# Attention and a pooled non-local block on two images: from eleven fenced stages to one program per engine

## The reference

```python
# layer 0: 8 heads of 32 channels
q, k, v = split(w_qkv @ X)                       # 256 x 4096 each
attn = softmax(q_h.T @ k_h / sqrt(32))           # 4096 x 4096 per head
X = w_proj @ (attn @ v_h) + X
# layer 1: non-local block with pooled keys (1024 = 4096 / 4) and values
g = maxpool2(g_w @ X + g_b)                      # 256 x 1024
theta = theta_w @ X[:64] + theta_b               # 64 x 4096
phi = maxpool2(phi_w @ X[64:] + phi_b)           # 64 x 1024
y = softmax(theta.T @ phi) @ g.T                 # 4096 x 1024, then 4096 x 256
X = batchnorm(W_w @ y.T + W_b) + X
```

## Time and profile before

| | |
|---|---|
| runs | 2638.99, 2633.73, 2636.41 us; median 2636.41 us |
| profiled execution | 2638.56 us, of which the span from first to last instruction is 2636.8 us |
| PE busy | 2511.5 us (95%) |
| ACT busy | 2285.4 us (87%) |
| DVE busy | 2176.7 us (83%) |
| POOL busy | 403.4 us (15%) |
| mean granted PE clock | 0.983 of 2.4 GHz |
| instructions | 59152 |
| instruction queues q8 and q14 | 202 packets with 3.31 MB and 86 packets with 0.70 MB |

### The profile page before, as it was taken

How to read it: one execution, slowest core, us unless ns; L and a number is a source line. 1 busy time by engine, 2 the same in 40 slices (tenths; PEclk the granted TensorE clock), 3 DMA queues, 4 the chain that set the end, 5 groups by cost and what they waited for, 6 DMA issues and landing times. The chain is left out here.

```text
span 2636.8 us, 59152 instructions
## 1 busy us (share of the span) xinstructions
PE 2511.5 (95%) x25066; PEld 722.6 (27%) x25066; DVE 2176.7 (83%) x1420; ACT 2285.4 (87%) x2575; POOL 403.4 (15%) x588
## 2 busy tenths in 40 slices
PE   6999999989999999898969999999899999998999
PEld 3222222232222222244432222222322222222444
DVE  5899999978899999696558999999689999996954
ACT  6999999979999999467469999999699999994664
POOL 0112211201112211110001221222011221121100
PEclk9999999999999999899989999999999999998999
DMA  2556656615556656201125666666155665662011
GB/s 86 113 129 126 125 120 129 126 37 111 115 129 126 125 120 129 56 1 49 42 73 129 122 126 124 126 125 124 30 113 129 126 125 120 129 126 43 1 56 40
DMA packets 85088, 262.65 MB, mean 100 GB/s; under 512 B 17616, under 2 KB 18704, under 8 KB 84528
## 3 DMA queue, kind: packets, MB, share of 16 engines
q0 software_dynamic: 64512, 234.91, 43.7%
q1 hardware_dynamic: 20288, 23.72, 2.7%
HBM read 14.75 MB, written 8.68 MB: 9 GB/s over the span
## 5 line engine op out<-in xcount | busy, mean ns | idle before, releaser
L542 DVE TENSOR_TENSOR acc<-acc,P 128x2048 f32<-128x2048 f32 x704 | 1613.4, 2292 | 79.9 <-ACT P L500 13.4
L500 ACT ACTIVATE P<-scores 128x1536 f32<-128x1536 f32 x1024 | 1596.1, 1559 | 0.0
L420 PE MATMUL psOL<-P,V 128*32 128x512 f32 (+1 forms) x8960 | 1073.1, 567 | 1.4 <-ACT P L500 1.4
L409 PE MATMUL psOL<-Q,K 32*128 32x512 f16 x3072 | 839.9, 379 | 28.8 <-ACT P L499 16.9
L409 PE MATMUL scores<-Q,K 32*128 32x512 f16 x9216 | 846.4, 379 | 0.0
L499 ACT ACTIVATE P<-psOL 128x512 f32<-128x512 f32 x1024 | 713.0, 696 | 36.6 <-PE scores L409 36.6
L567 POOL DMA_DIRECT2D accD<-P x384 | 335.6, 995 | 1229.3 <-ACT P L500 1046.2
L409 PEld LDWEIGHTS psOL<-Q,K 32*128 32x128 f16 x3072 | 207.0, 93 | 984.6 <-ACT P L499 856.5
L420 PEld LDWEIGHTS psOL<-P,V 128*32 128x32 f32 x8960 | 196.5, 108 | 473.9 <-issue 438.0
L409 PEld LDWEIGHTS scores<-Q,K 32*128 32x128 f16 x9216 | 220.0, 92 | 0.0
L564 POOL DMA_DIRECT2D accD<-P x64 | 35.2, 556 | 654.3 <-ACT P L500 371.9
(11 more groups left out here) (128 smaller groups left out, 1705.4 us busy)
## 6 DMA issues: line engine op xcount, KB each, us to landing
accD<-P POOLq DMA_DIRECT2D x448, 512.0 KB, 5.3
X<-in_x SPq DMA_DIRECT2D x16, 512.0 KB, 7.4
out<-res SPq DMA_DIRECT2D x32, 256.0 KB, 2.0
R<-pool_inv SPq DMA_DIRECT2D x2, 2048.0 KB, 7.0
wq<-in_w_qkv SPq DMA_DIRECT2D x1, 768.0 KB, 4.8
Ls<-L SPq DMA_DIRECT2D x32, 8.0 KB
att_inv<-Ls SPq DMA_DIRECT2D x32, 8.0 KB
ww_sb<-in_W_w SPq DMA_DIRECT2D x2, 256.0 KB, 2.8
```

The source lines that it names most:

```text
L409: last = nc.tensor.matmul(dst[h], K[rows, kp, j * 128:(j + 1) * 128], Q[rows, qp, cs], start=(n == 0), stop=(n == 2))
L420: last = nc.tensor.matmul(both[h * D:(h + 1) * D, lo:hi], V[:, j, h * D:(h + 1) * D], P[:, r + h, lo:hi], start=(j == 0), stop=(j == JT - 1))
L500: nc.scalar.activation(P[:, r + 1:r + G, :], bank[n % 2].rearrange("p (u n) -> p u n", n=CH), ACT.Exp, scale=SCORE).then_inc(s_exp, 1)
L542: nc.vector.tensor_tensor(acc[:], old, P[:, r:r + G, :], ALU.add).then_inc(s_add, 1)
```

## The change

There is one block for the whole of both images. Each stage is now a set of functions per engine (`Part`), and each engine runs through them in straight order, for b = 0 and b = 1 written out. Semaphores belong to the program; those of layer 0 and of layer 1 are cleared once by POOL in the middle of the other layer (`clean_first`, `clean_second`). All buffers that came and went are views of one arena with fixed places. The bounds of all four attentions go to `worst`; the flag is computed once at the end, and the branch to a general path that does both images again stands behind the end. At the borders parts are interleaved:

```diff
+        def sync_setup(sp):
+            sp.dma_start(wq32, wqkv.rearrange("(t p) o -> p t o", p=128)).then_inc(s_wq, 16)
+            for c in range(3):
+                load_x(sp, 0, c)
+            ...                       # the other weights, then X chunks 3 to 7
+        def scalar_setup(act):
+            act.wait_ge(s_wq, 16)
+            nc.scalar.activation(wq[0][:], wq32, ACT.Copy, scale=WS).then_inc(s_wqs, 1)
...
+                for c in range(NC):                    # projection, tensor
+                    unit(c, 0)
+                    if c == 0 and between:
+                        between(pe)                    # sums_of_acc, _tile, _dma of the attention before
...
+                low(0)                                 # projection, vector
+                if between:
+                    between(dve)                       # sums_out of the attention before, or results(NC - 1)
...
+                pe.wait_ge(s_nx, 2 * NC - 1)           # attention, tensor
+                pe.wait_ge(s_ev, 2 * NC - 2)
+                pe.wait_ge(s_ve, NC - 1)
+                scores(0, 0)
...
+            def room(act):                             # before Xh of the next projection is written
+                for m in range(NC * JT - RING, NC * JT - RING + 5):
+                    slot_free(act, m)
...
+                    if c == NC - 1 and following:      # attention, sync
+                        sp.wait_ge(s_ready, NC * JT)
+                        following(sp)                  # inverted sums of chunks 0 to 6 from DRAM
...
+                if between:                            # layer 1, tensor
+                    pe.wait_ge(behind.signals["exp"], 2 * NC * JT)
+                broadcast(0)                           # into two banks of scores6
+                if between:
+                    between(pe)                        # sums_of_acc, _tile, _dma
...
+                    if c == 1:                         # layer 1, vector: moved behind chunk 0
+                        for n in range(NG):
+                            dve.wait_ge(homes[n], 16 * NC if b is not None else 16)
+                        nc.vector.reciprocal(Ls[:, :, NC - 1, :], Ls[:, :, NC - 1, :]).then_inc(s_rec, 1)
...
+                for c in range(NC):                    # layer 1, sync
+                    for t in range(CT):
+                        sp.wait_ge(s_res, c * 2 + t + 1)
+                        sp.dma_start(out_v[dram, :, t, c * CH:(c + 1) * CH], res[:, t, :]).then_inc(s_st, 16)
+                    if following is not None:
+                        load_x(sp, following, c)
...
+            def _(act):
+                scalar_setup(act)
+                for b in range(B):
+                    if b:
+                        act.wait_ge(s_clean, CLEAN * b - 1)
+                        act.sem_inc(s_past, 1)
+                    project[0].scalar(act, 16 * (b + 1), None, (layer1.signals["yf"], CT * NC + 2) if b else None)
+                    if b == 0:
+                        scalar_weights(act)            # cw high, moved out of the setup
+                    attend[0].scalar(act)
+                    project[1].scalar(act, None, attend[0].signals["room"], None)
+                    attend[1].scalar(act)
+                    ...
+                    layer1.scalar(act, b)
...
+        end_phase(once + first_sems + layer1.sems)
+        known_safe = nc.values_load(safe[0:1, 0:1], min_val=0, max_val=1)
+        with nc.If(known_safe < 1):
+            with nc.Fori(0, B) as b:
+                general(b)
```

More of the change, by code:

```diff
@@ L1 @@
+from collections import namedtuple
 from contextlib import ExitStack
@@ new lines, in conv_seq @@
+        s_cw = sem(root, "s_cw")
+        s_sq0 = sem(root, "s_sq0")
+        s_bn = sem(root, "s_bn")
+        s_clean = sem(root, "s_clean")
+        s_past = sem(root, "s_past")
+        s_x = [sem(root, f"s_x{c}") for c in range(NC)]
+        loads = [(wp_sb[:], wproj.rearrange("(t p) o -> p t o", p=128)),
+                 (gw_sb, gw.rearrange("(t p) o -> p t o", p=128)),
+                 (col[:, :, 0:6], vectors.rearrange("(t p) k -> p t k", p=128)),
+                 (tb_sb[:], biases)]
@@ new lines, in gpsimd_setup, with vector_setup @@
+        def gpsimd_setup(pool):
+            nc.gpsimd.memset(ident[:], 0.0).then_inc(s_id, 1)
+            pool.wait_ge(s_id, 1)
+            nc.gpsimd.affine_select(out=ident[:], in_=ident[:], compare_op=ALU.not_equal, fill=1.0,
+                                    base=0, pattern=[[-1, 128]], channel_multiplier=1).then_inc(s_id, 1)
+        def vector_setup(dve):
+            nc.vector.memset(cw32[:, :, 0:CM], 0.0).then_inc(s_zero, 1)
+            nc.vector.memset(pw_sb[:, 0, :], 0.0).then_inc(s_zero, 1)
+            nc.vector.memset(ones[:], 1.0).then_inc(s_sp, 1)
+            nc.vector.memset(spread[:], 0.0).then_inc(s_sp, 1)
+            nc.vector.memset(heads[:], 0.0).then_inc(s_hd, 1)
+            dve.wait_ge(s_hd, 1)
+            for h in range(G):
+                last = nc.vector.memset(heads[h * D:(h + 1) * D, h * D:(h + 1) * D], 1.0)
+            last.then_inc(s_hd, 1)
+            dve.wait_ge(s_wqs, 1)
+            nc.vector.scalar_tensor_tensor(out=wq[1][:], in0=wq32, scalar=WS, in1=wq[0][:],
+                                           op0=ALU.mult, op1=ALU.subtract).then_inc(s_wqs, 1)
@@ new lines, in conv_seq, with clean_first, clean_second @@
+        project = [projection(g) for g in range(NG)]
+        attend = []
+        for g in range(NG):
+            attend.append(attention(g, project[g], attend[-1] if attend else None))
+        layer1 = second_layer(attend[-1], [a.signals["out"] for a in attend])
+        first_sems = [s for p in project + attend for s in p.sems]
+        def clean_first(pool):
+            for s in first_sems:
+                pool.sem_clear(s)
+            pool.sem_inc(s_clean, 1)
+        def clean_second(pool):
+            for s in layer1.sems:
+                pool.sem_clear(s)
+            pool.sem_inc(s_clean, 1)
@@ L1237, in layer1 @@
[L1237 to L1243 removed]
+                        layer1.signals["rows"](sp, b)
+                        for n in range(NG):
+                            sp.dma_start(Ls[:, n, NC - 1, :], L[0:128:D, :]).then_inc(attend[n].signals["out"], 16)
```

1865 lines of the change are left out of this document (971 added, 894 removed).

## The result

| | kernel before | changed kernel |
|---|---|---|
| median of the runs | 2636.25 us (2633.73 to 2638.99, 4 runs) | 2572.63 us (2569.51 to 2573.57, 4 runs) |
| profiled execution | 2638.56 us | 2573.04 us |
| its span | 2636.8 us | 2571.3 us |
| PE busy | 2511.5 us, 95% | 2501.2 us, 97% |

Ratio of after to before: 0.9756, 95% interval 0.9744 to 0.9767. The gain is 63.6 us by the medians and 65.5 by the two profiled executions; 74.9 were forecast. 2572.6 lies inside the range, 11.6 us above the predicted 2561 and just outside the likeliest case's own range (2552 to 2571).

The account below looks back on a forecast made before the run. Stages are bound by busy PE and ACT, so only PE's rests at borders can shrink: 11.0 + 6.9 + 18.9 + 25.4 + 18.1 = 80.3, less 5.4 gives 74.9 us, from median 2636.4 to 2561; range 2551 to 2580.

Parts of the forecast that it names:

- likeliest case: Whole kernel: the border gains come as reckoned, giving 2561 us, own range 2552 to 2571; chance 0.78.
- Start: Kernel's beginning, once: weights waited for singly and X loaded early, so PE starts at 9.0 instead of 19.97; gain 11.0 us.
- projection to attention: Four borders: scores wait only for an earlier reduction instead of a meeting, so exponentials start sooner; gain 6.9 us in all.
- image border: Image 0 to image 1, once: PE goes straight on at full clock with X already split; gain 18.1 us.
- Attention 0 to projection 1: Two borders: 17.5 us from last values to regular pace becomes 8.1, with flag and branch moved to the end; gain 18.9.
- Attention 1 to layer 1: Two borders: from last values to third residual 13.1 us instead of 26.4 and 25.2; gain 25.4 together.
- sums (3.1) to +4.4: Attention 1 to layer 1: after broadcast 0, the sums take 3.1 us and end 4.4 us behind the last values.
- End: After the last store: more clears 1.1 us, flag's load 0.5, jump over the general path 3.8; cost 5.4 us.
- the code, not the jump: Rival at stage borders: ACT's 3.8 us pause is fetching new code, which the straight program keeps; 2584 us, chance 0.06.
- loads before stores: Rival in image 0: queued X loads delay stores and so DVE and PE, 3 us per chunk; 2585 us, chance 0.04.
- partly: Rival: a wait at two of nine borders lasts as long as the meeting did, 10 to 14 us less; 2573, chance 0.08.
- the clock: Rival in the four attentions: unbroken PE work drops the clock to 1.2 GHz; 2677 us at 6%, chance 0.02.

Follow-up runs that it names:

- e7: Changed kernel with image 1's inputs loaded only after image 0's last store landed, and the last results ahead of the projection's first low part on VectorE; 2580.35 us.
- e4: Kernel before without its general path and the branch to it, stages and meetings as they were; 2620.21 us against 2638.11.
- e5: Changed kernel with the attention's sums put back ahead of the projection's first unit at the border from attention 0 to projection 1; 2568.92 us.
- e1: Changed kernel with the attention weights' rows of chunk 0 read back while attention 1's last chunk still runs; 2571.26 us.
- e10: e1 with rows of chunks 0 to 2 read at the start of attention 1's last chunk, 3 to 6 only behind the sums' copy; 2562.33 us.
- e3: Changed kernel without the general path, the branch and the flag's load at the end; 2565.41 us.
- e2: Changed kernel with the sums ahead of the first broadcast and chunk 0's normalisation behind the sums' copy, from attention 1 to layer 1; 2578.82 us.
- e9: e1 with tile 28 instead of 29 as the last tile that GpSimd's transfers add up in each chunk; 2570.40 us.
- e8: Changed kernel with e1's early rows, and the second broadcast and chunk 0's projection ahead of the third block of sums; 2564.11 us.
- e11: e8's order of work with e10's reads, and the last image's first-stage semaphores cleared by GpSimd within layer 1; 2558.66 us.
- e6: Changed kernel with four extra useless matmuls in each of the first three steps of every attention; 2573.30 us.

## Why the prediction was right, and where it was not

- *The number.* 2572.6 lies in the range of 2551 to 2580, but 11.6 us above the forecast and outside the likeliest case's own range (2552 to 2571). It is in by the width of the range: one term of the sum gave a third less than forecast.
- *What bounds the kernel; each border shifts all behind it.* Right: the busy times stood still and the ledger adds up (65.4 of 65.5).
- *Start, projection to attention, image border.* Right to 0.2 us. e7 shows that the image border's gain is 11.4 from overlap, which leaves 6.7 for what else went. The part that belongs to the general path (5.1 in e4) was in the measured border without my having seen it.
- *Attention 0 to projection 1.* Right (19.5, forecast 18.9), and "flag and branch go from here" too (4.7 and 4.9 of it by e4). The order of sums and unit is free, as e5 shows.
- *Attention 1 to layer 1.* Here the prediction failed, in the step "sums (3.1) to +4.4". The term 25.4 measured 16.9. I took the sums' length from a trace in which nothing ran beside GpSimd's last transfer (its third block starts at V + 2.8 before too), and moved the reads of the rows right beside it ("they go past nothing but SP's last `Ls` transfer"). I counted the queue that the reads are issued from, and not the transfers of another queue that are in flight beside them. The transfer landed at about V + 5.65 instead of V + 2.8 or earlier, and the low clock followed the waits for it and for the reads, which came at V + 1.3 (forecast 0.2). In image 0 it was the low clock that held the third block back to V + 6.29; with the reads' wait gone and the clock full (e1) the transfer still held it at V + 5.64, so nothing was won. With the reads elsewhere and nothing else changed (e10) res3 is at 12.9 in image 1 and 14.4 in image 0, on both sides of the forecast 13.1. The two add up to 27.3 against 26.2 by the forecast, so the sum's other members were sound to 1.1 us, which is low clock in image 0.
- *End.* 6.5 for 5.4: the jump took 4.5 instead of 3.8, and the span ended with PE's. The clears with the meeting behind them took 2.9 us (2563.2 to 2566.1) against 1.3 before (2635.2 to 2636.5), 1.6 more where 1.1 was forecast. The forecast scaled POOL's clears, but PE's end last: POOL is done at 2564.8, PE at 2566.0. e3 confirms load and jump with 5.1.
- *Of "the code, not the jump":* refuted by e4, where the pause goes with the branch. I had taken ACT's 3.8 us as the price of any jump. In the kernel before, that came near for PE too: its branches over the general path are recorded with 3.3 and 3.6 us, ACT's pause of 3.7 follows a record of 0.05. The 4.49 us at the end are PE's own, and what the other four engines paid there no trace shows. The equal price was my inference: the Trainium skill's "Advanced Engine Details and Errata", ISA Cache, gives no time, and it gives TensorE 128 KB where the other engines have 32. In "Runtime: NRT & Kernel Launch" (Instruction fetch mechanics) the skill says that a taken branch whose target is outside of the current window has to fetch before it goes on. PE's 4.49 us, ACT's pause and the nine instruction packets behind the last branches fit that. The packets of 16 KB that the prediction counted are those of q8 alone; q14's have 8 KB (86 with 0.70 MB).
- *Of "loads before stores":* refuted: the waits of `res` for stores are 17.5 us in all, 21.5 before. The sign named for it (over 4 us in image 0) was a poor one: it is 8.8 us there, but was 10.5 before the change too.
- *Of "partly":* it named 10 to 14 us lost at two borders because reads come late behind the scores. The size (8.5) and the place are near, the mechanism is another. The reads came 1.1 us later than reckoned, but to take that away won nothing (e1); they made something else late.
- *Of "the clock":* refuted for the long stretches (583 to 640: 1.00). What "no stretch under 0.9" left out are 16 us at three of the attentions' starts (0.79, 0.79, 0.89), and the 8 us of the border from attention 1 to layer 1 (1054 to 1062: 0.57).
- *The bounds.* The parts' own bounds add up to 2549 and 2589, not 2547 and 2592; the stated range doesn't hang on it.

## What to carry to other kernels

When a step is moved earlier, list not only the queue it is issued from but every transfer that is in flight at its new time, and who waits for the last of them: two reads of 48 KB made a 512 KB accumulation some 3 us later, and PE paid for it. A wait that the profile shows with 0.4 us can be the bound of a border, covered by work that happens to be slow; the test is to make the work ahead of it faster (e1, e2) and see whether the time comes back. A transfer that is issued for another tile also holds another buffer: see who asks for it next (e9). Where a wait can't go, put work of the next stage into it: that and the early rows brought 8 to 9 us here (e8), and with the transfers apart 13 (e11).

## What the runs showed of the hardware

- TensorE's compare-and-branch over the general path is recorded with 4.49 us (4.33 in e11, 3.41 in e6), that of the other four engines with 0.05 to 0.07. The short record hides a cost: in the kernel before, ScalarE stands for 3.7 us behind its own. At the changed kernel's end nine instruction packets follow the branches within 4.5 us.
- A general path that is never taken cost the loop of the kernel before 17.9 us, of which 5.1 lie at the image border, where only the loop's return jumps; SyncE's next DMA there came 4.3 us behind it, and 0.5 without the path.
- Two accumulating transfers of 512 KB with reads beside the later: 7.2 us to landing in the median instead of 5.6, all of it in the later one.
- PE's granted clock fell behind waits of 1 us in a row as well as behind one of 2.7, and not always in the same kernel: res3 in image 1 is at 17.7 and 20.6 in two executions of the same program.
